# Filler transposes on TensorE in front of four waits, none in steps 2 to 6, and the context copy ahead of the norm in the first steps

## The reference, cut to what matters

```
x   : (32, 128, 256)    ctx : (32, 128, 256)           float32, so 32 tiles of 128 tokens
q   = layernorm(x) @ Wq.T + bq      k, v = ctx @ Wk.T + bk, ctx @ Wv.T + bv
# each token: 16 heads of 16 numbers, attention over the heads of the same token
attn = softmax(q_i . k_j / 4)       x = x + (attn @ v) @ Wd.T + bd
# then 8 experts, top 1
gates = softmax(layernorm(x) @ w_red @ wg_n.T)         idx = argmax, score = max
x = x + score * (gelu(layernorm(x) @ W1[idx] + b1[idx]) @ W2[idx] + b2[idx])
```

## Time and profile before

| | |
|---|---|
| three runs, us | 369.04, 369.15, 372.51 |
| median, us | 369.15 |
| the profiled execution: its time, us | 374.02 |
| its span (first to last instruction), us | 372.2 |
| mean granted clock of TensorE in it | 0.958 |
| TensorE matmul busy | 342.1 us, 92% of the span |
| GpSimd busy | 284.4 us, 76% |
| VectorE busy | 259.5 us, 70% |
| ScalarE busy | 193.5 us, 52% |

### The profile page before, as it was taken

One profiled execution on the slowest core, in us unless ns is written; L12 is line 12 of the kernel. 1 busy time (PEld: TensorE's weight loads), 2 busy tenths in 40 slices (PEclk: granted clock), 3 DMA queues, 4 the chain that ended last, 5 costly groups with the idle time before them and its releaser, 6 DMA issues.

```text
span 372.2 us, 11172 instructions
## 1 busy us (share of the span) xinstructions
PE 342.1 (92%) x3755; PEld 293.3 (79%) x3755; DVE 259.5 (70%) x723; ACT 193.5 (52%) x525; POOL 284.4 (76%) x538
## 2 busy tenths in 40 slices
PE   7798699999999999896959989799999999999994
PEld 6587588888888888665647867689999999999993
DVE  6454778888888898888757556874666666666662
ACT  1001457788777777667765636413353535353431
POOL 3458769999999998877887487563777778888874
PEclk9899989999999999999588998987999999999999
DMA  6669997999999999989994112310122122222210
GB/s 216 202 204 257 282 251 214 264 254 273 266 261 271 302 312 320 341 238 239 269 400 162 28 48 82 95 59 29 59 73 74 62 67 73 65 68 73 61 48 1
DMA packets 55127, 63.87 MB, mean 172 GB/s; under 512 B 36526, under 2 KB 45887, under 8 KB 55072
## 3 DMA queue, kind: packets, MB, share of 16 engines
q1 hardware_dynamic: 50544, 52.77, 50.8%
q0 software_dynamic: 3744, 9.53, 8.7%
q10 hardware_dynamic: 784, 0.87, 0.7%
HBM read 42.00 MB, written 22.07 MB: 172 GB/s over the span
## 4 chain that ended last, share of the span: by engine, by line
PE 71%; DVE 10%; DMA 7%; POOL 5%; issue 4%; ACT 2%; DVEq 1%; SPq 0%; POOLq 0%; ACTq 0%
PE bQ L1144 16%; PE bL L1114 9%; PE bKV L1114 8%; PE bKV L949 6%; PE bQ L1039 6%; PE bKV L946 6%; PE bY L1002 6%; PE bO L969 4%; PE bL L958 3%; PE bT L1126 2%; DMA r<-row_scr,ig 2%; PE bA L1051 2%; DMA r<-in_xc 2%; DMA wA<-in_wqT 1%; DMA row_scr<-cat 1%
## 5 line engine op out<-in xcount | busy, mean ns | idle before, releaser
L1144 PE MATMUL bQ<-w,wA 128*128 x312 | 74.8, 383 | 3.6 <-DVE r L796 2.8
L1144 PEld LDWEIGHTS bQ<-w,wA 128*128 128x128 f32 x312 | 56.8, 192 | 11.1 <-issue 4.9
L396 POOL TENSOR_TENSOR x<-ql,mask 128x1024 f32<-128x1024 f32 x32 | 60.6, 1894 | 2.6 <-DVE r L655 0.4
L842 ACT ACTIVATE pad<-ql 64x512 f32<-64x512 f32 x64 | 40.1, 626 | 27.7 <-DMA ql<-qkv_scr 27.3
L427 POOL DMA_INDIRECT out<-r,isc x39 | 41.0, 1052 | 16.7 <-issue 12.5
L450 POOL DMA_INDIRECT r<-row_scr,ig x39 | 40.8, 1046 | 6.1 <-issue 2.0
L909 ACT ACTIVATE wA<-bL,r 128x128 f32<-128x128 f32 x76 | 21.7, 369 | 39.4 <-PE bL L1114 39.4
L1114 PEld LDWEIGHTS bL<-wA,r 128*128 128x128 f32 x304 | 39.9, 206 | 2.0 <-ACT wA L909 0.6
L1114 PEld LDWEIGHTS bKV<-wA,r 128*128 128x128 f32 x320 | 38.5, 192 | 3.2 <-issue 1.4
L1114 PE MATMUL bL<-wA,r 128*128 128x128 f32 x304 | 40.5, 291 | 0.4 <-ACT bX L829 0.4
L1114 PE MATMUL bKV<-wA,r 128*128 128x128 f32 x320 | 39.4, 276 | 1.4 <-DVE wA L783 0.8
(11 more groups left out here) (175 smaller groups left out, 667.0 us busy)
## 6 DMA issues: line engine op xcount, KB each, us to landing
qkv_scr<-qkv SPq DMA_DIRECT2D x16, 768.0 KB, 4.5
ql<-qkv_scr SPq DMA_DIRECT2D x32, 384.0 KB, 6.1
r<-in_xc SPq DMA_DIRECT2D x15, 512.0 KB, 5.7
row_scr<-cat SPq DMA_DIRECT2D x32, 133.5 KB, 6.4
w1b<-in_W1b SPq DMA_DIRECT2D x8, 514.0 KB, 7.2
w<-in_W SPq DMA_DIRECT2D x8, 512.0 KB
xt<-in_x SPq DMA_DIRECT2D x15, 256.0 KB, 5.8
b2b<-in_b SPq DMA_DIRECT2D x2, 512.0 KB, 9.4
```

The costliest lines, as they stand in the source:

```text
L396: eng.tensor_tensor(quarter(kx[:, z % 2, :]), spread(ql[z // 2 % 2][:, :, z % 2, 0:HD]), mask_k, ALU.mult).then_inc(S["kx"], 1)
L842: i_ = eng.activation(pad[n, z % 3, :].rearrange("p (k g h d) -> p k g h d", k=2, g=NG_, h=2) [:, :, :, h, :], ql[z // 2 % 2][n, :, z % 2, ...
L1144: i_ = eng.matmul(bQ[:, 0:C], hT[b % 2][:, k, :], w2[:, bass.ds(eb * (KH * C) + k * C, C)], start=(k == 0), stop=(k == KH - 1))
```

## The change

It moves GpSimd's context copy in front of the ve and the power in steps 0 to 4 (in step -1 and from step 5 on the order stays). It takes away the three filler transposes at the end of each of steps 2 to 6. It adds filler transposes into bank bT: 16 in steps 7 and 32 and 8 in step 35, each just ahead of the values matmuls (L969) and their wait for the expanded probabilities, and 12 in step 36 ahead of the first turned rows (L1126).

```diff
+FILLS = {7: 16, 32: 16, 35: 8}
+FILLS_ROWS = 12
...
@@ pool_attention
                 if t == -1:
                     pool_norm(eng)
-                    pool_context(eng, 0)
+                if not live(z):
+                    pool_context(eng, t + 1)
                 if live(n) or live(d):
...
-                if t >= 0 and not live(z):
-                    pool_context(eng, t + 1)
                 if t == 0:
                     pool_constants(eng)
...
@@ tensor_attention
                 if t == FIRST + 2:
+                    fill(eng, FILLS_ROWS, bT)
                     tensor_rows(eng, 1)
...
                 if live(a) and t >= 8:
                     tensor_project(eng, a)
+                fill(eng, FILLS.get(t, 0), bT)
                 if live(s1):
                     eng.wait_ge(S["axv"], by_vector(s1))
                     eng.wait_ge(S["axs"], by_scalar(s1))
...
-                if t < 7:
+                if t < 2:
                     fill(eng, 3, bA)
```

## The result

| | before | after |
|---|---|---|
| median of 22 runs each, us | 371.22 (368.12 to 375.41) | 367.58 (364.61 to 371.60) |
| ratio, 95% interval | | 0.9909 (0.9884 to 0.9935) |
| profiled execution: time, span, us | 374.02, 372.2 | 368.67, 366.9 |
| mean granted clock in it | 0.958 | 0.976 |

The change makes the kernel faster by 0.65 to 1.2%, 2.4 to 4.3 us. I forecast 5.1 us off 369.15; 22 runs of the kernel before have a median 2.1 us above that of the first three.

What follows compares the result with a forecast made beforehand. TensorE, 71% of the last-ending chain, was taken as the bound, slowed by waits and low clock. 3.5 + 0 + 1.7 + 0.4 + 1.3 = 6.9 us, discounted to 5.1, off 369.15 gave 364.0 us; range 360.3 to 368.8.

Steps and rivals of the forecast that it cites:

- Part 1: Steps 0 to 4, context copy first: loads go out earlier and K of tile 6 starts 3.1 to 3.9 us earlier, taken as 3.5.
- the discount for runs that lack the first low stretch: Part 1: up to 1.7 of the 3.5 us is the first low stretch, perhaps absent in median runs; 0.8 us taken off.
- Part 2: Steps 2 to 6 without fillers: taken as 0, with 0 to 3.4 us of possible loss from two low stretches.
- rival D: Steps 2 to 6: unfilled load waits drop the clock, up to all of tiles 4 to 7 slow, 372.7 us; chance 0.04.
- Part 3, step 7: 16 fillers ahead of the values of step 7 avoid the low stretch at 47.3 us: 1.7 us gained.
- Part 3, whether transposes keep the clock up: The gains at all four filler places assume that transposes hold TensorE's clock up; the rows were said not to settle it.
- Rival B: Transposes don't count for the clock, so only the context copy gains: 366.4 us, range 365.2 to 368; chance 0.28.
- Part 3, steps 32, 35 and 36: Late fillers avoid low clock: 0.4 us (0 to 1) in step 32, 1.3 us in steps 35 and 36.
- The base: The time of the kernel before, 369.15 us, from which the forecast took off 5.1 us.

Runs made afterwards that it cites:

- e3: The changed kernel with the three filler transposes at the end of each of steps 2 to 6 put back; 366.47 us, ratio 0.9871.
- e1: The kernel before with only the context copy moved first in steps 0 to 4, early fillers kept, none added; 368.73 us, ratio 0.9924.
- e6: The kernel before without the filler transposes of steps 2 to 6, nothing else changed; ratio 0.9999.
- e8: The changed kernel with 40 transposes in the setup instead of 16; one profile, in which the 40 take 6.28 us.
- e2: The kernel before with only the added fillers of steps 7, 32, 35 and 36 (16, 16, 8 and 12); ratio 0.9994.
- e5: The changed kernel with 20 transposes at the end of step 5, ahead of the wait for context tiles 6 and 7; 366.34 us, ratio 0.9849.
- e14: The changed kernel itself, timed again beside a version without the fillers of steps 32, 35 and 36; 368.17 us, ratio 0.9945.
- e15: The kernel before with only the fillers of steps 32, 35 and 36 added; 370.83 us, ratio 1.0023.
- e12: The changed kernel with 24 transposes instead of 12 ahead of the first turned rows; one profile, 318.65 us from the projection of step 9 to the end.
- e4: The changed kernel itself, timed again on the chip of the first group of experiments; 367.03 us, ratio 0.9895.

## Why the prediction was right or wrong

- **Part 1 was right.** I forecast 3.1 to 3.9 us and took 3.5. From K of tile 0 to K of tile 6 it is 26.3 us in the mean of the five profiles with the copy behind and 22.8 in the 13 with the copy first: 3.5 us. (Read from the span's start it is 4.75 us in the two main profiles, of which 1.0 is K of tile 0 itself, at 9.03 us in that of before.) Alone it has a ratio of 0.9924, 2.8 us (1.6 to 4.1). What was late next came as worked out: the constants, then the copy of tile 2 right behind (17.17), then the loads. The load of tiles 4 and 5 went out at 16.51 us where I had 18.2; 1.0 of that is the start. So tile 4 had no wait at all, and the whole wait moved to tile 6. Two details were wrong. I counted 0.65 us in the 3.5 for the fillers of steps 2 and 3; the load of tiles 6 and 7 goes out at 23.59 us with them (e3) and without them, and K of tile 6 comes at 22.8 us either way, so they give nothing and the copy gives all. And the discount for runs that lack the first low stretch isn't borne out: all five profiles with the copy behind have it, and e1 gains 3.8 us in the span where its profile gains 4.0 up to step 7.
- **Part 2 was the first step that failed.** I took 0 with a loss of 0 to 3.4 us. The loss was 1.1 us in the mean of the profiles (a fall that costs 1.5 to 1.8 us in four of six), and the mechanism is the one of my rival D at a tenth of its price: one wait instead of four tiles. I had the reason in the text, that the waits grow without anything in them, but put both of them at up to 1.6 us. The wait at step 4 vanished, and that at step 6 got all 1.3 us that the fillers of steps 2 to 5 had taken: 2.0 to 2.8 us in six profiles with the copy first, and 2.41 in e6 with the copy behind.
- **Part 3, step 7: right in size.** 1.68 us measured where the clock would fall, 1.7 forecast; of four profiles without the filler it fell in three.
- **Part 3, whether transposes keep the clock up: right.** They do: e8 decides that they raise it, and the 14 profiles with the filler of step 7 that they hold it. Rival B and the rule of the Trainium skill behind it ("TensorE: Matmul & The Clock Gate", section "Part 4: PE-mode transpose") fall: here float32 transposes raised the clock and held it. The matmuls at 6.31 us in the earlier trace rows, which I took for it, only came too early.
- **Part 3, steps 32, 35 and 36: the second step that failed, the term that I put too high.** I forecast 0.4 and 1.3 us, 1.7 in all; the spans give 0.8 us (0.2 to 1.5) for the three groups together. The local reading was right: the projection went from 1.97 to 1.06 us, and the first to the second turned rows took 4.84 to 4.90 us in ten profiles with the clock up, 5.3 to 6.6 in six with a low one (two more have the clock up and 5.5 and 6.2). But 16 transposes in step 32 often only shift the fall by a step or two (e2, e5, e14, e15). Between 165 and 200 us the clock is low for 10.7 us in the mean of the seven profiles without late fillers and for 2.8 in the eleven with them, so 8 us less of low clock were worth less than one. Where the rest goes is not settled. That the second rows wait for a gather was tried in e12 and isn't it.
- **A term that I left at nothing: the time beyond the span.** I took the 1.8 us of the kernel before as fixed. In the changed kernel it is 2.4 us in the mean, 0.6 us of the gain. Why is open.
- **The base.** 369.15 us was the median of three; of 22 it is 371.22. Of the 3.6 us between 364.0 and the measured 367.58, 2.1 are this. I explained the distance of the profiled execution (374.02) by low clock alone; 1.4 us of it is the late start of tile 0 (9.03 us against a mean of 7.6 in 16 other profiles, e8 with its 40 transposes left out).

Summed anew: 3.8 (copy, with the fillers kept, up to the logits of step 7: 33.2, the mean of the five with the copy behind, less 29.4) - 1.1 + 1.3 (1.68 us in three of four) + 0.8 = 4.8 us of span, against 4.5 (3.9 to 5.1) measured. Less the 0.6 us beyond the span it is 4.2 us, against 2.4 to 4.3 in time. The forecast of 5.1 lay 0.8 to 2.7 us too high.

## What to carry to other kernels

Filler work ahead of a wait pays where TensorE is full and on the path behind it (step 7: 1.7 us), and little where the work behind waits for other engines anyway, however long the low stretch looks in the clock line (late fillers: 8 us less of low clock, 0.8 us of time). When work is taken away ahead of a wait for a load, ask whether the load comes earlier too: where it doesn't, the wait grows by all of that work, and whatever filled it is missed now. With runs that differ by 1% and a change of 1%, compare profiles between marks, but only where the mark is steady: one interval told 1.68 us to 0.02, while the long one from step 9 to the end varies by 4 us and hid 0.8. And compare spans beside times: a kernel can lose outside its span what it gained inside.

## What the runs showed of the hardware that I had not expected

- Transposes alone raise TensorE's clock from 1.2 to 2.4 GHz: within 40 of them the record fell from 421 to 272 ns (e8).
- At the start of the trace the granted clock reads 1.00 while records are at 1.2 GHz: the 16 transposes at 1.67 us take 421 ns each. The trace's clock records begin only at 9.70 us in the profile of before and at 7.75 in that of the changed kernel, which is where the records shorten (matmuls of K from 634 to 380 ns, transposes from 421 to 273); with no clock record the line shows 1.00. Until then the length of a known record tells the clock.
- The falls differ between executions of one kernel. The same wait of step 6 had a low stretch behind it in the changed kernel and e14 and none in e4; step 28 had one in e3, e4 and e12 alone. The mean granted clock of single executions of the changed kernel went from 0.971 to 0.997, and their times from 371.6 to 364.6 us.
- The time beyond the span isn't the same for all kernels: 1.7 to 1.9 us in most, up to 3.9 in the changed kernel.
